# Two products of q and k moved into the softmax, and the sixth and seventh steps reordered, in an adaLN block with log-sparse attention

## What is computed

```
mod = (silu(c) @ wmod): six rows of 256 for each sample: sa, ca, ga, sb, cb, gb
ga, gb are kept at least 0.25 away from zero
h = layernorm(x) * (1 + ca) + sa
x = x + ga * attention(h)          # 16 heads of 16; query i sees key i and the keys i - 1, i - 2, i - 4, ... i - 256
h = layernorm(x) * (1 + cb) + sb
x = x + gb * (quantised(h) @ quantised(Wf).T + bf)   # blocks of 32: scale = max|h| / 7.5, values on a 6-bit grid
```

## Time and profile before

| | us |
|---|---|
| median of 3 runs | 280.79 |
| lowest, highest | 279.94, 280.97 |
| the profiled execution, its own time | 280.1 |
| its span, first to last instruction | 278.3 |
| PE busy | 253.6 (91% of the span) |
| DVE busy | 249.4 (90%) |
| ACT busy | 210.8 (76%) |
| POOL busy | 209.4 (75%) |

### The profile page before, as it was taken

The page is one execution under the profiler, slowest core; times in us unless marked ns, Lnnn a source line. Parts: engine busy times, 40 slices in busy tenths (PEclk is TensorE's granted clock), DMA queues, the critical chain, the costliest instruction groups (busy, mean ns, idle before and its releaser), DMA issues.

```text
span 278.3 us, 4396 instructions
## 1 busy us (share of the span) xinstructions
PE 253.6 (91%) x1356; PEld 162.7 (58%) x1356; DVE 249.4 (90%) x318; ACT 210.8 (76%) x564; POOL 209.4 (75%) x159
## 2 busy tenths in 40 slices
PE   6999996999999998799999999999999578997885
PEld 1754565258636843485568654766468445895664
DVE  3699899989998999999889998999984999999970
ACT  2377896785888896989889997998776736666753
POOL 6201339996998999999999899999999899945100
PEclk9999997999999999999999999999999999999999
DMA  7752996696695489327944796069803875730006
GB/s 226 191 194 78 297 312 179 205 351 196 212 320 182 141 273 319 127 98 252 341 143 132 221 361 197 19 204 364 247 1 116 255 212 180 227 133 15 0 5 224
DMA packets 54386, 53.90 MB, mean 194 GB/s; under 512 B 4094, under 2 KB 52812, under 8 KB 54364
## 3 DMA queue, kind: packets, MB, share of 16 engines
q1 hardware_dynamic: 54364, 53.63, 60.4%
HBM read 44.89 MB, written 8.72 MB: 193 GB/s over the span
## 4 chain that ended last, share of the span: by engine, by line
DVE 32%; PE 30%; ACT 14%; POOL 13%; issue 8%; DMA 1%; DVEq 0%; POOLq 0%; ACTq 0%
POOL pv_buf L681 7%; DVE prod L1758 6%; DVE pv_buf L1894 5%; PE ps L847 5%; PE ps L1111 5%; DVE prod L1894 4%; PE ps L1032 4%; DVE prod L1747 4%; PE ps L980 3%; ACT x_norm L1217 3%; ACT dump L1240 2%; PE ps L876 2%; POOL h L394 2%; POOL x_norm L389 2%; PE ps L834 2%
## 5 line engine op out<-in xcount | busy, mean ns | idle before, releaser
L681 POOL TENSOR_TENSOR pv_buf<-pv_buf 128x1024 f32<-128x1024 f32 x48 | 113.8, 2370 | 5.0 <-DVE pv_buf L1894 0.8
L1758 DVE TENSOR_TENSOR prod<-ps,kT 128x1024 f32<-128x1024 f32 (+4 forms) x70 | 75.0, 1107 | 0.0
L1894 DVE TENSOR_TENSOR pv_buf<-v_shift,ps 128x1024 f32<-128x1024 f32 x49 | 59.0, 1209 | 1.0 <-POOL pv_buf L681 1.0
L876 PE MATMUL ps<-wT,h_cen 128*128 128x256 f32 x128 | 29.9, 379 | 0.0
L847 PE MATMUL ps<-hT,wT 128*128 128x512 f32 x64 | 29.6, 603 | 0.0
L858 PE MATMUL ps<-hT,wT 128*128 128x512 f32 x64 | 29.4, 599 | 0.0
L876 PEld LDWEIGHTS ps<-wT,h_cen 128*128 128x128 f32 x128 | 23.9, 190 | 6.4 <-issue 3.8
L980 PE MATMUL ps<-prod,sel_sum 128*32 128x512 f32 x208 | 25.0, 598 | 2.0 <-DVE prod L1758 1.5
L1032 PE MATMUL ps<-wo_g,w_raw 128*128 128x256 f32 x112 | 26.4, 379 | 0.0
L662 POOL TENSOR_TENSOR rstd<-var,minus_half 128x4 f32<-128x4 f32 x8 | 8.1, 1017 | 20.5 <-ACT var L1244 19.0
L1032 PEld LDWEIGHTS ps<-wo_g,w_raw 128*128 128x128 f32 x112 | 21.2, 190 | 3.5
(11 more groups left out here) (220 smaller groups left out, 570.7 us busy)
## 6 DMA issues: line engine op xcount, KB each, us to landing
v_shift<-v_rows SPq DMA_DIRECT2D x56, 512.0 KB, 5.5
x_in<-in_L_attn_x SPq DMA_DIRECT2D x8, 512.0 KB, 4.0
v_rows<-v_base SPq DMA_DIRECT2D x8, 512.0 KB, 3.0
x_res<-in_L_attn_x SPq DMA_DIRECT2D x8, 512.0 KB, 6.1
out_x<-outb SPq DMA_DIRECT2D x5, 512.0 KB, 4.7
rows_mod<-mod_rows SPq DMA_DIRECT2D x7, 256.0 KB, 6.1
x<-in_L_wmod SPq DMA_DIRECT2D x1, 1024.0 KB, 8.1
row_ga<-mod_rows SPq DMA_DIRECT2D x8, 128.0 KB, 3.0
```

What stands on the lines that cost most here:

```text
L681: nc.gpsimd.tensor_tensor(dst, dst, ring(b, n)[:, t:NT, :], ALU.add).then_inc(s_add, 1)
L876: mm = nc.tensor.matmul(ps23[:, k2, col:col + D], h_cen[:, k, P * t:P * t + P], wT[:, 2, k, :], start=(t % 2 == 0 and k == 0), stop=(t % 2 ...
L1758: nc.vector.tensor_tensor(prod[:, n, :, o:L], ps01[:, :, o:L], kT[:, b % 2, :, 0:L - o], ALU.mult).then_inc(s_prod, 1)
L1894: nc.vector.tensor_tensor(dst[:, at, :].rearrange("p t (h e) -> p t h e", e=DH), v_n.rearrange("p t (h e) -> p t h e", e=DH), weights, ALU ...
```

## The change

In steps 3 to 5 DVE's order becomes: maximum, reciprocal of the kept scales, scores less maximum, quantise, weights less exp(-max), their sum, qk product 0, reciprocal of the sum, qk product 1, weights' product, and then the products of v from number 0 on. The block maxima of b - 2 are split in `block_peaks` and `peaks_to_scales`, and where products 8 and 9 of v are DVE's (steps 3 to 5) they stand between the two. In step 6 the block maxima and the quantisation of sample 4 move behind product 3 of v.

POOL does `gate_ffn(b - 3)` ahead of `add(b, 1)`. In step 5, `rstd_after(4)` moves from behind add 5 to behind add 3, and `gate_projection(5)` from behind add 7 to ahead of add 6.

PE and ACT take the second half of v's rows of sample 7 ahead of `xd` of sample 3. On ACT, `norm_after(4)` moves from step 6 (behind `exps(6)`) to step 5, ahead of `copy_scores(6)`, and `exps(6)` stands ahead of `quantised(3)`.

POOL, steps 0 to 5:

```diff
+                if has(b - 3):
+                    gate_ffn(b - 3)
                 add(b, 1)
                 if has(b - 2):
                     modulate(pool, nc.gpsimd, b - 2)
-                if has(b - 3):
-                    gate_ffn(b - 3)
                 add(b, 2)
                 add(b, 3)
+                if not has(b + 3):
+                    rstd_after(b - 1)
                 add(b, 4)
                 add(b, 5)
                 if has(b + 3):
                     rstd_before(b + 3)
                 else:
-                    rstd_after(b - 1)
+                    gate_projection(b)
                 add(b, 6)
                 if not has(b + 3):
                     dequantise_early(b - 2)
                 add(b, 7)
-                gate_projection(b)
+                if has(b + 3):
+                    gate_projection(b)
```

PE, step 6:

```diff
             v_rows(LAST, 1)
+            v_rows(LAST, 0)
             xd_transposes(LAST - 4)
-            v_rows(LAST, 0)
             attention_transposes(LAST - 2)
```

ACT, the end of the loop's body, then step 6:

```diff
+                if not norm1:
+                    norm_after(b - 1)
                 copy_scores(b + 1)
                 if ahead:
                     seed_q(b + 2)
 
+            exps(LAST - 1)
             quantised(LAST - 4)
-            exps(LAST - 1)
-            norm_after(LAST - 3)
             evacuate_v(LAST, 1)
+            evacuate_v(LAST, 0)
             evacuate_xd(LAST - 4)
-            evacuate_v(LAST, 0)
```

DVE, `block_maxima` in two functions, whose bodies are as before:

```diff
             def block_maxima(b, half_=None):
+                block_peaks(b, half_)
+                peaks_to_scales(b, half_)
```

DVE, in `softmax_weights`:

```diff
-                link(nc.vector.tensor_reduce(z_sum, w_rest.rearrange("p t s h -> p t h s"), AX_X, ALU.add))
-                link(nc.vector.reciprocal(z_inv[:, :, :], z_sum))
+                nc.vector.tensor_reduce(z_sum, w_rest.rearrange("p t s h -> p t h s"), AX_X, ALU.add).then_inc(s_sm, 1)
+                if 3 <= b < LAST - 1:
+                    qk_product(b + 1, 0)
+                dve.wait_ge(s_sm, NSM * b + 2)
+                nc.vector.reciprocal(z_inv[:, :, :], z_sum).then_inc(s_sm, 1)
+                if 3 <= b < LAST - 1:
+                    qk_product(b + 1, 1)
+                dve.wait_ge(s_sm, NSM * b + 3)
```

DVE, steps 0 to 5:

```diff
                 softmax_max(b)
                 if has(b - 3):
                     invert_scales(b - 3)
+                softmax_less_max(b)
+                if has(b - 3):
                     quantise(b - 3)
                 softmax_weights(b)
                 pv_product(b, 0)
                 pv_product(b, 1)
-                qk(b, 0)
+                if b < 3:
+                    qk(b, 0)
                 pv_product(b, 2)
-                qk(b, 1)
+                if b < 3:
+                    qk(b, 1)
                 pv_product(b, 3)
...
                 pv_product(b, 7)
+                if has(b - 2):
+                    block_peaks(b - 2)
                 if b >= EARLY:
                     pv_product(b, 8)
                     pv_product(b, 9)
                 if has(b - 2):
-                    block_maxima(b - 2)
+                    peaks_to_scales(b - 2)
```

DVE, step 6:

```diff
             qk(b, 0)
-            block_maxima(LAST - 3)
-            quantise(LAST - 3)
             pv_product(b, 2)
             qk(b, 1)
             pv_product(b, 3)
+            block_maxima(LAST - 3)
+            quantise(LAST - 3)
             qk(b, 2, 3)
```

More of the change, by code:

```diff
@@ L1761, in block_maxima, with block_peaks @@
             def block_maxima(b, half_=None):
+                block_peaks(b, half_)
+                peaks_to_scales(b, half_)
+            def block_peaks(b, half_=None):
                 t, g, _ = halves(half_)
-                n = upto_half(b, half_)
-                src, (peak, scale, inv) = h2_by[b], block_scales(b)
+                src, peak = h2_by[b], block_scales(b)[0]
                 made, n_made = step_of(b, half_, s_h2, s_h2l)
@@ L1768, in block_maxima, with peaks_to_scales @@
                                         ALU.max, apply_absolute_value=True).then_inc(s_post, 1)
+            def peaks_to_scales(b, half_=None):
+                g = halves(half_)[1]
+                n = upto_half(b, half_)
+                peak, scale, inv = block_scales(b)
                 dve.wait_ge(s_post, NPOST * n - 2)
@@ L1834, in softmax_max, with softmax_less_max @@
                                         ALU.max).then_inc(s_max, 1)
+            def softmax_less_max(b):
+                scores = scores_in(ps67 if b < LAST else ps23)
                 dve.wait_ge(s_max, b + 1)
@@ L1865, in softmax_weights @@
                     nc.vector.tensor_tensor(w, w, per_head(z_inv, NS), ALU.mult).then_inc(s_w, 1)
-                assert k[0] == NSM
+                assert k[0] == NSM - 2
             def pv_product(b, n):
@@ L1960, in _ @@
             softmax_max(LAST)
+            softmax_less_max(LAST)
             softmax_weights(LAST)
```

## The result

The changed kernel takes 281.17 us (median of 20 runs, 279.94 to 282.49) against 280.41 us for the kernel before (20 runs, 279.72 to 280.99). The ratio is 1.0028, 95% interval 1.0017 to 1.0039: slower by 0.5 to 1.1 us. The forecast was a median of 280.2 us, 0.6 us faster. The profiled execution took 282.15 us, its span is 280.2 us and its granted clock 0.988 on average; before it was 280.1, 278.3 and 0.994.

The account below looks back on a forecast made before the run. All four engines were taken as busy 27.1 to 29.0 us of a 29.5 us step. Gains and delays through steps 3 to 7, capped by POOL's scaling in the tail, left 0.6 us: 280.79 - 0.6 = 280.2 us, range 278.6 to 282.0.

Parts of the forecast that it names:

- Bounds: Whole loop: four engines nearly full in 29.5 us steps; the only large wait aimed at is DVE's 3.70 us for `h2`.
- DVE's softmax: DVE, steps 3 to 5: closed gaps save 0.59 us a step, hidden by the wait for scores in steps 3 and 4.
- POOL: POOL, steps 3 to 5: gate ahead of add 1 fills a wait; adds that started at 189.84 start 0.5 us earlier.
- steps 5 and 6: POOL waits 2.1 us in step 5, step 6 starts 0.7 us later; DVE's `h2` wait falls from 3.70 to 0.8.
- PE's lateness: PE, step 6: attention transposes 2.5 us later, at 210.7 instead of 208.20; its 2.00 us wait for ACT's seed follows.
- the rule weighed there: Skill's DRAIN rule: next DVE operation waits until the pipe is empty, so DVE's softmax saving would be 0, not 0.59 us.
- Both signs: Wrong if POOL does not wait at `rstd_after(4)`, or if PE's late work reaches the scores of sample 7.
- The later subtraction: Softmax: scores less maximum starts 1.08 us after the maximum instead of 0.93, ACT 0.15 us late, in steps 4 and 5.
- The row of `gate_ffn(4)`: SP's queue, step 6: this row goes out 1.1 us later, sent at 216.2, needed at 220.9; cost nothing, up to 0.3.
- The tail: Behind step 7: `shift_sixth`, capped by POOL's scaling of sample 6, starts at 252.65; the end comes 0.6 us earlier.
- Slower: the norm ahead of the scores: Rival, steps 6 and 7: PE's late transposes not taken up by its waits, step 7 1.8 us later, 282.6; chance 0.14.
- The gain gets through: Rival: POOL's wait at `rstd_after(4)` is small, DVE's 2.2 us or more arrive, about 278.5; chance 0.27.

Follow-up runs that it names:

- e3: Kernel before with only the steps 3 to 5 part: DVE's new order, split block maxima, FFN gate ahead of add 1; 279.67 us, ratio 0.9970.
- e6: Changed kernel with scores less maximum again right behind the maximum, ahead of the kept scales' reciprocal; 280.41 us, ratio 0.9994 to the kernel before.
- e1: Changed kernel with POOL's last FFN gate held until DVE has done `shift_sixth`; 280.23 us, ratio 0.9986 to the kernel before.
- e9: Changed kernel with ACT's `norm_after(4)` back in step 6 behind the exponentials; 280.9 us, ratio 1.0038 to the kernel before.
- e2: Changed kernel with five small matmuls filling PE's idle time ahead of the tail's transposes of xd of sample 5; 280.8 us, ratio 1.0003 to the kernel before.
- e4: Kernel before with only the reordering of steps 5 to 7, steps 3 and 4 and the softmax as before; 280.56 us, ratio 1.0001.
- e7: Kernel before plus steps 3 to 5 part (subtraction first), sample 4's block maxima and quantisation behind v product 3, last gate behind `shift_sixth`; 278.73 us, ratio 0.9935.
- e11: Kernel before plus steps 3 to 5 part (subtraction first) and sample 4's block maxima and quantisation behind v product 3, last gate not held; 278.7 us, ratio 0.9949.
- e12: Second run of the kernel before with only sample 4's block maxima and quantisation moved behind product 3 of v in step 6; 279.62 us, ratio 0.9971.
- e5: Kernel before with POOL's last FFN gate held until DVE has quantised sample 5, to start together with `shift_sixth`; 280.94 us, ratio 1.0011.

## Why the prediction was wrong

Each of its places is set beside the trace, less the 0.35 us of the late start:

| the prediction's step | forecast | measured |
|---|---|---|
| maximum to weights' subtraction | 2.96 us | 2.91 |
| POOL's new wait at `rstd_after(4)` | 2.1 us | 2.06 |
| `norm_after(4)` ends | 199.7 | 199.64 |
| step 6 starts | 201.5 | 201.34 |
| `modulate(4)` starts | 210.1 | 210.04 |
| attention transposes of PE | 210.7 | 210.59 |
| DVE's wait for `h2` | 0.8 us | 0.77 |
| qk products 2 and 3 | 218.0 | 217.89 |
| PE's FFN half | 220.75 | 220.71 |
| head sums | 228.75 | 228.53 |
| step 7 starts | 233.4 | 233.16 |
| `shift_sixth` starts | 252.65 | 252.70 |
| end of the span | 277.7 | 279.85 |

The measured median, 281.17 us, lies inside the range of 278.6 to 282.0; that is owed to the range's width, not to the reasoning.

- **Bounds, DVE's softmax, POOL, steps 5 and 6, PE's lateness:** right, each to 0.25 us. By the rule weighed there DVE's saving would have been 0; it is not, since `e3` comes to step 6 0.62 us earlier and is 0.4 to 1.3 us faster. The Trainium skill, "VectorE: DVE Perf Modes", section "The DRAIN you can't avoid", adds that a next operation which is not held starts earlier. The prediction left this out; the overlap of 0.08 us agrees with it. Both signs by which the prediction would have known itself wrong (POOL not waiting at `rstd_after(4)`, PE's lateness in the scores of sample 7) stayed away: the fault lay where it had set none.
- **The later subtraction:** taken at 0.15 us a step, it measured 0.10 in step 4 (`e6`).
- **The row of `gate_ffn(4)`, "nothing, up to 0.3":** no wait in the changed kernel's profile, but 0.50 and 0.85 us in those of `e1` and `e9`. The bound was too small.
- **The tail, "DVE takes up `shift_sixth` at 252.65, and the end comes 0.6 us earlier": this is the step that failed.** The start was right. The prediction then took for granted that the end follows the start. It kept `shift_sixth` at its old length without a word, though it had just found what releases it: POOL's scaling, behind which POOL itself goes on to `gate_ffn`. Two things stood between. PE's projection of sample 7 lets the statistics start only 0.16 us earlier than before (`e6`); and beside the gate the shift takes 2.27 us, which costs 0.53 us on that path. So -0.57 became -0.16 and then +0.37: the statistics start 0.37 us later than before, where the prediction's 0.6 us earlier would have had to arrive. The collision is shown by the table of overlaps, and its price on the path by the rows of six profiles that have it and one that has not. How often it comes in the changed kernel's 20 runs is not known (`e6`, with the same tail, escaped it once), and the times of `e1` and `e2` do not show the 0.53 us.
- **The clock, not in the prediction at all.** A fall in the tail costs about 1 us. Among the 20 runs of the changed kernel eight have a mean clock of 0.988 and take 281.79 us on average, three have 0.994 (281.01) and nine 0.999 or more (280.66). But the kernel before has such runs too: 28 of the 90 that ran beside the first eleven experiments are under 0.990 (one run of 429.5 us is left out), and in the set beside `e1` to `e4` they take 281.28 us where the other 20 take 280.3. Eight of 20 is not clearly more than 28 of 90; the three sets differ much among themselves (13 of 33, 10 of 28, 5 of 29), and in `e9` it is six of 12 beside that last five of 29. So that the change brings the fall on is neither shown nor excluded; the profile's 1.18 us is mostly an execution's luck, and its part in the median's 0.76 us is not known. The nine runs at 280.66 are 0.3 to 0.5 us over the three sets of the kernel before without such runs (280.32, 280.32, 280.13), and the trace gives 0.37. But these sets ran beside other kernels, and `e2`, which differs from the changed kernel by five small matmuls, has 280.15 in its six such runs, below its own set's 280.32. How the 0.76 us divide between the two causes is therefore open.
- **The rivals.** "Slower: the norm ahead of the scores" had the right sign and the wrong place: PE's lateness was taken up by its waits, as forecast, and `e9` shows that nothing is won by the norm's old place. "The gain gets through" is what `e7` and `e11` do, with POOL's wait taken away, as its condition said.

## What to carry to other kernels

When an instruction is forecast to start earlier, ask what runs beside it at its new place, above all when one event releases two engines at once; and ask which other input it or its successor waits for, since the gain ends at the first of these. A power moved ahead on one engine gained nothing here, since the value it needs was made 2 us later on another: look up that row first, as the whole queue behind it waits too. Take a change apart before it is judged: here one half was worth 0.8 us, and the other, worth nothing alone, took it back.

## What the runs showed of the hardware

- A DVE instruction with two SBUF inputs (`shift_sixth`, 128x1024) and a POOL multiplication of SBUF operands (128x512) run one after the other. Whoever starts second is longer by the overlap less 0.14 us: 0.24 us of overlap gave 0.10, 1.20 gave 1.06, and it holds for either engine in second place. The timeline shows the wait as length of the instruction (2.27 us for 1.22), not as idle time in brackets. The Trainium skill, "SBUF — State Buffer", section "SBUF: two separate sides", states this: GpSimd and a DVE instruction with two SBUF inputs share a pair of ports under an exclusive lock, whoever starts first has it for its whole instruction, and the other is blocked. The trace agrees. In the loop DVE's products, which take one input from PSUM, run beside POOL's adds at 1.21 to 1.22 us each, and the adds at 2.35 to 2.38.
- PE's granted clock fell in some executions in one or two of three places and not in others of the same kernel: 0.83 from 40 to 50 us, 0.66 from 220 to 225, 0.66 to 0.75 from 260 to 265, the second behind an idle time of PE of 2.01 us, which stood in the same place in `e12`, where the clock stayed at full. The first cost nothing that the times show, the second 1.45 us at step 7 in one profile and nothing in another (that of `e5`, where DVE was still behind), the third about 1 us. Filling PE's idle time in the tail did not keep it away, by the clocks and times of the runs of `e2`. One profile is not enough to price a wait for PE: look at the granted clock of its window first.
